# Down weight loaded into its low half's place and split a turn later, with a new order in the first three turns of pass two

## What is computed

```python
x = x + autocorrelation(layernorm(x), ctx, ctx)            # FFT correlation, top 8 lags
x = x + layernorm(x) @ W.T + bias + lora                   # 8 adapters of rank 16
x = x + attention(layernorm(x), ctx, ctx)                  # 32 query heads, 8 key/value heads of 16
h = relu(xn @ up_w) ** 2                                   # xn = layernorm(x), up_w 512 x 1024
x = x + layernorm(h @ down_w + routed(xn), gamma, beta)    # down_w 1024 x 512
```

## Time and profile before

| | |
|---|---|
| median of 3 runs | 705.79 us (703.43 to 708.24) |
| the profiled execution | 702.67 us, span 700.9 us |
| mean granted TensorE clock | 0.985 |
| busy: PE, DVE, ACT, POOL | 95%, 71%, 60%, 53% |
| PE busy in slices of 17.5 us, in tenths | 8789999999989788899999999999999999999986 |
| chain that ended last | PE 78%, DVE 12%, issue 3%, ACT 2%, POOL 2% |

### The profile page before, as it was taken

How to read it: one execution, slowest core, us unless ns; L and a number is a source line. 1 busy time by engine, 2 the same in 40 slices (tenths; PEclk the granted TensorE clock), 3 DMA queues, 4 the chain that set the end, 5 groups by cost and what they waited for, 6 DMA issues and landing times.

```text
span 700.9 us, 12436 instructions
## 1 busy us (share of the span) xinstructions
PE 663.5 (95%) x3898; PEld 481.3 (69%) x3898; DVE 496.9 (71%) x1123; ACT 421.5 (60%) x773; POOL 373.6 (53%) x461
## 2 busy tenths in 40 slices
PE   8789999999989788899999999999999999999986
PEld 3445555555556466687887787878877878787775
DVE  4678788888876687477776776777767767775444
ACT  4548787868647763846647558367475584674221
POOL 1547998987766425245454653454545534544451
PEclk9789999999999999999999999999999999999999
DMA  8223444353234421202222113021221230211000
GB/s 263 90 81 115 144 127 151 122 166 106 60 106 119 136 74 35 76 30 61 58 65 60 37 53 90 30 60 56 64 60 33 56 90 30 60 23 53 16 16 30
DMA packets 32118, 54.36 MB, mean 78 GB/s; under 512 B 5296, under 2 KB 7088, under 8 KB 32080
## 3 DMA queue, kind: packets, MB, share of 16 engines
q1 hardware_dynamic: 32080, 53.90, 25.9%
HBM read 36.84 MB, written 8.39 MB: 65 GB/s over the span
## 4 chain that ended last, share of the span: by engine, by line
PE 78%; DVE 12%; issue 3%; ACT 2%; POOL 2%; DMA 1%; SPq 1%; DVEq 0%; POOLq 0%; ACTq 0%
PE wide L1228 7%; PE wide L1230 6%; PE wide L1229 6%; PE ps_b L1228 6%; PE ps_b L1230 5%; PE ps_b L1229 5%; PE ps_b L1273 4%; PE bank L1340 4%; PE ps_a L1273 4%; PE wide L1330 4%; PE ps_b L1412 4%; DVE gmax L1053 2%; PE ps_a L1228 2%; PE ps_a L1230 2%; DVE x_in L928 2%
## 5 line engine op out<-in xcount | busy, mean ns | idle before, releaser
L746 POOL TENSOR_TENSOR va<-mv,small 128x1 f32<-128x1 f32 x80 | 15.4, 193 | 158.2 <-DVE mv L1207 79.3
L716 ACT ACTIVATE stage<-wide 128x512 f32<-128x512 f32 x30 | 16.3, 595 | 83.3 <-PE bank L1513 83.3
L832 POOL TENSOR_TENSOR y_l<-y,y_h 128x512 fp32r<-128x512 f32 x16 | 20.6, 1288 | 71.2 <-ACT y_h L618 71.2
L1077 DVE RECIPROCAL y<-ps_b 128x256 f32<-128x256 f32 x32 | 55.9, 1748 | 0.0
L1228 PE MATMUL wide<-up_h,t_h 128*128 128x512 f32 x128 | 52.3, 408 | 1.7 <-DVE t_l L1163 1.7
L641 ACT ACTIVATE probs<-wide 128x1024 f32<-128x1024 f32 x32 | 32.8, 1026 | 34.0 <-PE wide L1466 34.0
L1230 PE MATMUL wide<-up_h,t_l 128*128 128x512 f32 x128 | 50.8, 396 | 0.0
L1229 PE MATMUL wide<-up_l,t_h 128*128 128x512 f32 x128 | 50.3, 393 | 0.0
L1228 PE MATMUL ps_b<-down_h,ht_h 128*128 128x512 f32 x120 | 49.6, 413 | 0.4 <-DVE ht_l L1151 0.4
L748 POOL TENSOR_TENSOR rs<-va,small 128x1 f32<-128x1 f32 x80 | 44.5, 556 | 6.3
L1230 PE MATMUL ps_b<-down_h,ht_l 128*128 128x512 f32 x120 | 47.1, 393 | 0.0
(11 more groups left out here) (227 smaller groups left out, 2131.5 us busy)
## 6 DMA issues: line engine op xcount, KB each, us to landing
q_stack<-qt_h SPq DMA_DIRECT2D x128, 64.0 KB, 2.0
x_in<-in_x SPq DMA_DIRECT2D x16, 256.0 KB, 2.7
ctx_t<-in_ctx SPq DMA_DIRECT2D x16, 256.0 KB, 2.6
x_res<-in_x SPq DMA_DIRECT2D x16, 256.0 KB, 2.8
x_in<-x_rows SPq DMA_DIRECT2D x16, 256.0 KB, 2.6
ctx_t<-in_ctx_turned SPq DMA_DIRECT2D x16, 256.0 KB, 2.9
x_res<-x_rows SPq DMA_DIRECT2D x16, 256.0 KB, 3.0
out<-stage SPq DMA_DIRECT2D x15, 256.0 KB, 3.0
```

Source lines behind the costliest of these rows:

```text
L1077: dve.reciprocal(y[:, :, b, :], part[:, 1]).then_inc(S["den_s"], 1)
```

## The change

Each part of the down weight gets a buffer of its own, `down_raw0` and `down_raw1`, that lies where its low half will lie; the low half is subtracted in place. Three semaphores of `stage2` become three of the down weight, and the waits on `stage2` fall away. The split moves: part 0 from `turn_one` (ACT, DVE) to `turn_two` (ACT) and `body2(-1)` (DVE), part 1 from `turn_two` to `body2(-1)`. The load of part 1 now stands behind the last store of `x2` and waits for all four merges. Beside that, calls in `turn_one`, `turn_two` and `body2(-1)` change places on every engine.

```diff
-        down_h[0], down_l[0] = sb("down_h0", [P, DC * D], F32R), sb("down_l0", [P, DC * D], F32R)
+        def down_weight(c):
+            down_h[c] = sb(f"down_h{c}", [P, DC * D], F32R)
+            with ExitStack() as tmp:
+                down_raw[c] = sb(f"down_raw{c}", [P, DC * D], stack=tmp)
+            down_l[c] = sb(f"down_l{c}", [P, DC * D], F32R)
...
+        def opening(i):
+            return isinstance(i, int) and i == -1
...
             def turn_two():                                        # SP
                 stacked(1)
-                down_load(1)
                 store(LAST)
                 for stored in x2_stored:
                     sp.wait_ge(stored, 8 * NT)
+                sp.wait_ge(S["rt_ps"], DC)
+                down_load(1)
...
                 query_high(1)                                      # ACT, turn_one
+                layer_in(LAST)
                 guard_rows(0)
-                layer_in(LAST)
                 weights_of(0, 0)
-                down_high(0)
                 weights_of(0, 1)
...
                 queries_stacked(1)                                 # ACT, turn_two
+                merged_high(3)
                 guard_rows(1)
                 query_high(2)
-                merged_high(3)
                 weights_of(1, 0)
-                act.wait_ge(S["x2_s"], NT)
-                for stored in x2_stored:
-                    act.wait_ge(stored, 8 * NT)
-                down_high(1)
+                down_high(0)
                 weights_of(1, 1)
...
-                query_high(i + 4)                                  # ACT, body2
-                guard_rows(i + 3)
+                if opening(i):
+                    guard_rows(2)
+                    query_high(3)
+                    down_high(1)
+                else:
+                    query_high(i + 4)
+                    guard_rows(i + 3)
...
                 keys_spread(0)                                     # POOL, turn_one
+                layer_low(LAST)
                 layer_sum(LAST - 1)
-                layer_low(LAST)
...
                 rstd(0, mv4, va4, rs4, 4)                          # POOL, turn_two
+                third_beta(0)
...
                 queries(1)                                         # DVE, turn_one
-                down_low(0)
...
                 attended(0)                                        # DVE, turn_two
+                merged_low(0)
                 maxima(1, 0)
                 context_low(2)
+                merged_low(1)
                 maxima(1, 1)
                 normalised(2)
-                merged_low(0)
+                merged_low(2)
                 third(0)
-                merged_low(1)
-                merged_low(2)
                 values(1)
                 keys_values(2)
+                merged_low(3)
                 third_norm(0)
-                merged_low(3)
                 queries(2)
-                down_low(1)
...
                 attended(i + 2)                                    # DVE, body2
+                if opening(i):
+                    down_low(0)
...
                 keys_values(i + 4)
+                if opening(i):
+                    down_low(1)
...
                 rough_scores(1, 1)                                 # PE, turn_two
+                pe.wait_ge(S["rt_lo"], 1)
+                merge(3)
                 output(0)
                 turned_maxima(1)
-                pe.wait_ge(S["rt_lo"], 1)
-                merge(3)
...
-                keys_values(i + 4)                                 # PE, body2
-                turned_maxima(i + 3)
+                if opening(i):
+                    turned_maxima(2)
+                    keys_values(3)
+                else:
+                    keys_values(i + 4)
+                    turned_maxima(i + 3)
```

More of the change, by code:

```diff
@@ L205, in build @@
         ht_h, ht_l = sb("ht_h", [P, D], F32R), sb("ht_l", [P, D], F32R)
-        down_h, down_l = [None, sb("down_h1", [P, DC * D], F32R)], [None, sb("down_l1", [P, DC * D], F32R)]
+        down_h, down_l, down_raw = [None] * 2, [None] * 2, [None] * 2
+        def down_weight(c):
[3 more added lines that the diff above has]
+            down_l[c] = sb(f"down_l{c}", [P, DC * D], F32R)
+        down_weight(1)
         x3, xn4 = sb("x3", [P, D]), sb("xn4", [P, D])
         k_pairs = xn4[0:GUARD].rearrange("r (p n) -> r p n", p=PAIRS)
-        down_h[0], down_l[0] = sb("down_h0", [P, DC * D], F32R), sb("down_l0", [P, DC * D], F32R)
+        down_weight(0)
         qt_h, qt_l = sb("qt_h", [P, D], F32R), sb("qt_l", [P, D], F32R)
@@ L228, in build @@
         bn5, mv5, va5, rs5 = (sb(n, [P, w]) for n, w in (("bn5", 6), ("mv5", 2), ("va5", 1), ("rs5", 1)))
-        SEMS = """stage2_in stage2_hi stage2_lo vbd_zero
+        SEMS = """down_in down_hi down_lo vbd_zero
             tile_loaded ctx2_loaded res2_loaded out_stored
@@ L441, in down_load @@
             def down_load(c):
-                wait(sp, S["stage2_lo"], c)
-                sp.dma_start(stage2[:].rearrange("p (c n) -> p c n", c=DC), down_v[:, DC * c:DC * (c + 1), :]
-                             ).then_inc(S["stage2_in"], 16)
+                sp.dma_start(down_raw[c][:].rearrange("p (c n) -> p c n", c=DC),
+                             down_v[:, DC * c:DC * (c + 1), :]).then_inc(S["down_in"], 16)
             def residual(t):
@@ L644, in down_high @@
             def down_high(c):
-                act.wait_ge(S["stage2_in"], 16 * (c + 1))
-                act.activation(down_h[c][:], stage2[:], ACT.Copy).then_inc(S["stage2_hi"], 1)
+                act.wait_ge(S["down_in"], 16 * (c + 1))
+                act.activation(down_h[c][:], down_raw[c][:], ACT.Copy).then_inc(S["down_hi"], 1)
             def merged_high(c):
@@ L710, in body2 @@
                 if live(t):
-                    if isinstance(t, int) and t == 0:
-                        act.wait_ge(S["stage2_lo"], 2)
                     wait(act, *((S["pv_ps"], 2 * NT) if final(t) else (S["ht_ps"], 2 * t)))
@@ L849, in keys_spread, with third_beta @@
                                        .to_broadcast([GUARD, 2 * PAIRS, 2, SEQ]), ALU.mult).then_inc(S["kbd_s"], 1)
+            def third_beta(t):
+                if live(t):
+                    pool.wait_ge(S["x3_s"], t + 1)
+                    wait(pool, S["x3c_s"], t)
+                    pool.tensor_tensor(x3b[:], x3[:], beta_all[:], ALU.add).then_inc(S["x3b_s"], 1)
             def turn_one():
@@ L880, in body2 @@
                     rstd(t, mv3, va3, rs3, 3)
-                t = i + 1
-                if live(t):
-                    pool.wait_ge(S["x3_s"], t + 1)
-                    wait(pool, S["x3c_s"], t)
-                    pool.tensor_tensor(x3b[:], x3[:], beta_all[:], ALU.add).then_inc(S["x3b_s"], 1)
+                if not opening(i):
+                    third_beta(i + 1)
                 keys_spread(i + 3)
@@ L1110, in down_low @@
             def down_low(c):
-                dve.wait_ge(S["stage2_hi"], c + 1)
-                dve.tensor_tensor(down_l[c][:], stage2[:], down_h[c][:].bitcast(F32), ALU.subtract
-                                  ).then_inc(S["stage2_lo"], 1)
+                dve.wait_ge(S["down_hi"], c + 1)
+                dve.tensor_tensor(down_l[c][:], down_raw[c][:], down_h[c][:].bitcast(F32), ALU.subtract
+                                  ).then_inc(S["down_lo"], 1)
             def turn_one():
@@ L1517, in down @@
                 pe.wait_ge(S["ht_lo"], 2 * t + part + 1)
+                if isinstance(t, int) and t == 0:
+                    pe.wait_ge(S["down_lo"], part + 1)
                 high, low = ht_of(t, part)
@@ L1554, in body2 @@
                 if live(t) and not final(t):
-                    if isinstance(t, int) and t == 0:
-                        pe.wait_ge(S["stage2_lo"], 2)
                     wait(pe, S["y_s"], capped(2, t + 3))
```

## The result

| | before | after |
|---|---|---|
| median | 706.82 us (4 runs, 703.43 to 708.24) | 695.28 us (4 runs, 690.39 to 696.76) |
| profiled execution, span | 702.67, 700.9 us | 690.39, 688.6 us |
| granted clock of the span | 0.985 | 0.994 |

The time is 0.9857 of before, 95% interval 0.9808 to 0.9907: 1.4% faster, some 10 us. In a second comparison (six runs of the changed kernel, median 694.42), it is 0.9859 (0.9818 to 0.9900). The forecast was 697.4 us within 693.8 to 701.2 and a gain of 8.4.

The account below looks back on a forecast made before the run. PE was taken to bound the kernel; its holes plus a clock fall, 15.8 us before, less 7.5 of holes after, gave a gain taken as 8.4: median 705.79 to 697.4 us, range 693.8 to 701.2.

Parts of the forecast that it names:

- What bounds the kernel: PE, busy 389.15 of 400.9 us from 300 us on; time its list gains before 287 us should survive.
- The first load: turn_two: without ACT's 4.85 us wait for the down weight transfer, rough_scores(1,0) starts 4.0 us earlier.
- Rest of turn_two: merge(3) fills PE before output(0); new 0.5 wait for x3; products_kv(2) at 245.1 (250.25 before), queries 5.4 earlier.
- The lock between DVE and POOL: body2(-1): down_low(0) holds up POOL's y_l; output(1) waits 1.0; without it the sum would be about 0.5 larger.
- x3b: body2(-1): tile 0's x3b is done at 248, not 272.60; hole before the routed product 0.6 instead of 3.15.
- The early turned maxima: body2(-1): turned_maxima(2) ahead of the keys waits 1.45 for DVE, whose normalisation of tile 3 POOL's k_stack holds.
- The peak of 9.7 and the loss at `x_l` and `q_sb`: body2(-1): scores 9.7 earlier; then a 0.8 hole before the queries, q_sb 0.3 late; tile 3's query transposes 8.6 earlier.
- The sum: Holes and clock before 15.8, holes after 7.5, gain taken as 8.4; median 705.79 to 697.4 us, 1.2% faster.
- the term of the clock, 1.3: After the 3.09 us hole twelve matmuls take 2.73 us at clock 0.50, 1.45 at 1.00: 1.3 gained.
- Rival 2: Clock falls in the string of holes from 262.3 to 274; gain only 6.4 to 7.1, 699.0 us; chance 0.12.
- Rivals 1, 3 and 4: DVE chain longer, 700.4 (0.17); slower engine takes back lead after 300, 705.8 (0.05); SP's loads late, 713 or above (0.03).

Follow-up runs that it names:

- `b_fill`: Kernel before plus unread matmuls filling three of PE's holes (6, 11 and 9), no wait removed; ratio 0.9953 (0.9921 to 0.9984).
- `b_x3b`: Kernel before with one edit: POOL adds x3b of tile 0 at the end of turn_two; ratio 0.9969 (0.9934 to 1.0003).
- `a_split_early`: Changed kernel with both down weight parts split at the old places, turn_one and turn_two; queries(1) to tile 3's queries 62.05 us, not timed.
- `a_best2`: `a_max_first` with down_low(0) behind keys_values(3) and down_low(1) in body2(0); queries(1) to tile 3's queries 55.15 us, not timed.
- `a_max_first`: Changed kernel with DVE's maxima(2,1) ahead of tile 3's normalisation in body2(-1); queries(1) to tile 3's queries 54.56 us, not timed.
- `a_tm_late`: Changed kernel with the old order of turned maxima/keys and guard rows/x_h in body2(-1); queries(1) to tile 3's queries 56.51 us, not timed.
- `a_x3b_late`: Changed kernel with x3b of tile 0 back at its old place in body2(-1); queries(1) to tile 3's queries 56.84 us, not timed.
- `b_down`: Kernel before with only the down weight part (buffers, loads, places of its split), other calls in old order; ratio 0.9937 (0.9906 to 0.9968).

## Why the prediction was right

Its steps beside the trace of after, both counted in us from the first product of `queries(1)` (222.96 in the times of the prediction, 219.50 after):

| start of | forecast | measured |
|---|---|---|
| `rough_scores(1,0)` | 10.7 | 10.87 |
| `products_kv(2)` | 22.1 | 22.30 |
| `queries(2)` | 25.7 | 25.82 |
| up product, tile 0 | 31.8 | 32.20 |
| `output(1)` | 40.3 | 40.39 |
| routed product, tile 0 | 44.1 | 44.23 |
| `turned_maxima(2)` | 47.2 | 47.33 |
| scores, tile 2 | 49.8 | 50.23 |
| tile 3's queries turned | 55.1 | 55.53 |

- *What bounds the kernel*: right. PE's lead of 8.28 us at 275 is 8.84 at the end; nothing took it back. Of the small waits on `x3` behind it there were five before and one or three in the two executions of after.
- *The first load*: right in kind, 10.87 against 10.7. Its size differs between executions: in four with the early split ACT waited 4.85 (before), 4.8 (`b_fill`), 6.1 (`b_x3b`) and 5.6 us (`a_split_early`) for the transfer. In the last two PE's hole was 2.50 and 3.01 us in place of 1.28, and the clock fell behind it. The change removes that too, and the sum has nothing for it.
- *Rest of turn_two*: right, with the new wait of 0.44 for `x3`. `merge(3)` ahead of the output is worth 1.4, shown by its undoing, where I expected 0.5. The prediction cites the earlier trace rows for the wait before, but its line is not there; it is shown with that experiment.
- *The lock between DVE and POOL*: right, `y_l` is held up by 1.3. PE is idle 0.52 for it, some 0.75 by the count of the prediction, where 1.0 was forecast: the up product came 0.4 later than in my chain. That it cost 0.5 in the end was not borne out: where `a_best2` takes it away, the stretch is 0.6 longer than with it, through another wait between the same two engines; so the price of this one alone stays open.
- *x3b*: the hole is 0.46 where 0.6 was forecast. Undoing it costs 1.3. On the kernel before it gains 3.5 between the up product and the scores, but two falls of the clock took that back in the profiled execution, and the timed gain, 2.2, has an interval that just reaches zero.
- *The early turned maxima*: the hole of 1.42 against 1.45 is there, and behind `k_stack` as said (the normalisation of tile 3 takes 0.96 beside it, and 0.54 in `a_max_first`, where it stands later).
- *The peak of 9.7 and the loss at `x_l` and `q_sb`*: right (9.3 and 8.3).
- *The sum*: 8.4 forecast, 8.28 in the stretch, 8.8 to the end of the trace. The median moved by 11.5, the ratio by 10. What is mis-sized is the term of the clock, 1.3. It was read from one execution with one fall; the filled holes show some 3.3 us in the mean. The timed runs divide the gain. At a granted clock of 0.986 seven runs of before average 702.43 and three of the changed kernel 696.37: 6.1 us at an equal clock, where the prediction has 7.1 for the waits and 7.1 are found in the two traces (8.28 less 1.2). The mean clock is 0.9833 over 45 runs of before and 0.9903 over ten of the changed kernel, and the other 4 us of the 10 go with that. So in the timed runs the waits came out a little smaller and the clock some three times as large; that these two errors offset each other in part is luck. Part of the difference in clock may be chance in pass one, which the change doesn't touch.
- *Rival 2*, the clock falling in the string of holes: not seen in the two profiles of the changed kernel, nor in six of kernels one or two edits away from it. It did fall there in `a_tm_late`, where a hole of 2.49 us is left, and in `a_split_early`, near 280, where the longest is 1.91. In `a_x3b_late` a hole of 2.27 is left there, and it held. So the rival is possible, and the runs don't say how often it comes. Rivals 1, 3 and 4 did not come; the second load took 5.3 us and nobody waited for it.

## What to carry to other kernels

Walk the bounding engine's list through the new order with the durations of the old trace, and keep the chains of the other engines beside it: at each meeting point the later one counts, and an edit's worth is what is left at the last one. A copy of a constant that waits for a transfer belongs where nothing urgent stands behind it on its engine; how long it delays them depends on when the transfer lands, and one profile shows only one landing (6.9 to 9.9 us for the first part in these executions). Before an edit moves one engine's operation, look at what the other one of DVE and POOL runs at that time: `a_best2` took one such wait away and met another. Before pricing a hole, look at several executions: a fall of the clock behind it can add 1 us or more, and where a hole can't be removed, filling it with idle matmuls kept the clock here.

## What was not expected of the hardware

- Behind holes of TensorE of about 2.3 to 3 us its granted clock fell from 2.4 to 1.2 GHz in some of these executions and not in others: 2.49 us without a fall (before) and with one (`a_tm_late`), 2.27 without (`b_down`, `a_x3b_late`), 2.48 without (`b_down`), 2.30 with (`b_x3b`), 2.50, 3.01 and 3.09 with. Each kernel with such a hole was profiled once, so what belongs to the kernel and what to the execution is not told apart. In `a_split_early` it fell near 280 us too, behind holes of 0.85 and 1.91. The Trainium skill (TensorE: Matmul & The Clock Gate, Why this matters for your kernels) warns of idle gaps between bursts; the trace agrees, but by these runs the length of a single gap does not settle it.
- A fall of some 3 to 4 us cost 1.0 to 1.7 us here where PE is fed behind it: 1.0 (`a_tm_late` against the changed kernel), 1.2 (before against `b_fill`), 1.3 (the routed product of before), 1.65 (`b_x3b` behind the scores).
- Pass one, untouched by all these kernels, takes from 219.5 to 228.4 us up to `queries(1)`, at mean clocks of 0.98 and 0.95. The clock is low there between 10 and 60 us above all (0.67 to 0.88 in slices of 10 us in `a_max_first`). The two profiled executions of the changed kernel differ by 4.0 us, 3.85 of them in this part; what decides it was not studied.
